# Mamba mixer and mixture of experts on one core: the recurrence's products, the squares and two weight copies moved to GpSimd, the first tap and the output projection moved ahead

## What is computed

```python
def _rmsnorm(x, w, eps=1e-05):
    return x * jax.lax.rsqrt(jnp.mean(x * x, axis=-1, keepdims=True) + eps) * w

def _mamba2_layer(h, Wi, cw, cb, dtb, Alog, Dh, gw, Wo):
    zxbcdt = h @ Wi
    z, xBC, dt = jnp.split(zxbcdt, [D_INNER, D_INNER + CONV_DIM], axis=-1)
    xp = jnp.pad(xBC, ((0, 0), (D_CONV - 1, 0), (0, 0)))
    conv = cb + sum((xp[:, k:k + L, :] * cw[:, k] for k in range(D_CONV)))
    xBC = jax.nn.silu(conv)
    ...
    def step(hs, inp):
        dA_t, dtx_t, B_t, C_t = inp
        hs = hs * dA_t[:, :, None, None] + dtx_t[..., None] * B_t[:, None, None, :]
        y = jnp.einsum('bhpn,bn->bhp', hs, C_t)
        return (hs, y)
    ...
    y = ys.swapaxes(0, 1) + Dh[None, None, :, None] * xs
    y = _rmsnorm(y * jax.nn.silu(z), gw)
    return y @ Wo

for l in range(N_LAYER):
    h = h + _mamba2_layer(_rmsnorm(h, block_norm_w[l]), W_in[l], conv_w[l], conv_b[l], ...)
```

## Time and profile before

| what | value |
|---|---|
| median of 3 runs | 1160.88 us (1157.63 to 1161.12) |
| profiled execution | 1162.99 us, span 1161.0 us |
| mean granted clock of TensorE | 0.952 |
| PE busy | 993.7 us (86%) |
| DVE busy | 977.1 us (84%) |
| ACT busy | 884.2 us (76%) |
| POOL busy | 676.3 us (58%) |

### The profile page before, as it was taken

How to read it: one execution, slowest core, us unless ns; L and a number is a source line. 1 busy time by engine, 2 the same in 40 slices (tenths; PEclk the granted TensorE clock), 3 DMA queues, 4 the chain that set the end, 5 groups by cost and what they waited for, 6 DMA issues and landing times.

```text
span 1161.0 us, 25184 instructions
## 1 busy us (share of the span) xinstructions
PE 993.7 (86%) x6136; PEld 559.7 (48%) x6136; DVE 977.1 (84%) x1801; ACT 884.2 (76%) x1724; POOL 676.3 (58%) x853
## 2 busy tenths in 40 slices
PE   5799999999899999999999999985788767999980
PEld 4244544445444444454445444542444445777760
DVE  6779999999999999999999998974778775888865
ACT  5688999999899999999999999984556534655640
POOL 0267577766776677656655765672244551666661
PEclk9789999999999999999999999998888888999995
DMA  5111242224222432210001000100000115676638
GB/s 141 34 34 33 89 156 86 88 87 153 91 86 87 142 102 86 78 32 22 22 23 31 22 22 23 27 7 1 19 28 28 37 33 180 223 232 226 223 116 217
DMA packets 85584, 97.84 MB, mean 84 GB/s; under 512 B 20698, under 2 KB 65888, under 8 KB 85536
## 3 DMA queue, kind: packets, MB, share of 16 engines
q1 hardware_dynamic: 80544, 88.83, 24.2%
q0 software_dynamic: 4992, 8.48, 2.2%
HBM read 59.67 MB, written 37.83 MB: 84 GB/s over the span
## 4 chain that ended last, share of the span: by engine, by line
PE 35%; DVE 26%; issue 18%; ACT 6%; POOL 3%; DVEq 2%; DMA 1%; ACTq 0%; SPq 0%; POOLq 0%
DVE cv L1354 9%; PE bank L494 4%; PE bank L562 4%; PE bank L681 2%; PE bank L667 2%; DVE M L1370 2%; PE bank L683 2%; PE bank L682 2%; DVE cv L1350 2%; PE bank L619 2%; PE bank L693 2%; PE bank L695 2%; PE bank L692 2%; PE bank L658 2%; PE bank L640 2%
## 5 line engine op out<-in xcount | busy, mean ns | idle before, releaser
L1354 DVE SCALAR_TENSOR_TENSOR cv<-bank,PAR,cv 128x511 f32<-128x511 f32 (+2 forms) x384 | 274.1, 742 | 15.7 <-ACT cv L963 2.8
L1370 DVE SCALAR_TENSOR_TENSOR M<-E,bank 128x512 f32<-128x512 f32 x256 | 168.3, 678 | 20.7 <-ACT E L951 11.4
L1679 POOL TENSOR_TENSOR yt<-yt,ti 128x384 f32<-128x384 f32 x64 | 64.0, 1000 | 203.6 <-DVE ti L1470 203.6
L494 PE MATMUL bank<-hn,WA 128*128 128x512 f32 x256 | 144.9, 649 | 41.0 <-DVE cv L1354 40.6
L951 ACT ACTIVATE E<-bank 128x512 f32<-128x512 f32 x256 | 149.0, 595 | 31.9 <-DVE M L1370 30.1
L1710 POOL DMA_INDIRECT RS<-y,XR x92 | 98.8, 1074 | 78.7 <-DVE y L1567 55.4
L1703 POOL DMA_INDIRECT XS<-stage,IDX x64 | 65.9, 1029 | 79.2 <-DVE run L1329 62.1
L1101 ACT ACTIVATE hr<-bank,W1B 128x512 f32<-128x512 f32 x92 | 63.4, 689 | 56.7 <-PE bank L683 49.8
L562 PE MATMUL bank<-M,dtx 128*32 128x128 f32 x2048 | 82.9, 279 | 15.6 <-DVE o_sb L1389 15.1
L494 PEld LDWEIGHTS bank<-hn,WA 128*128 128x128 f32 x256 | 40.6, 194 | 111.9 <-issue 74.0
L1497 DVE TENSOR_TENSOR hL<-hr,hH 128x512 fp32r<-128x512 f32 x124 | 87.1, 702 | 4.3
(11 more groups left out here) (245 smaller groups left out, 2633.8 us busy)
## 6 DMA issues: line engine op xcount, KB each, us to landing
XS<-PADT SPq DMA_DIRECT2D x32, 520.0 KB, 4.3
WA<-w_in SPq DMA_DIRECT2D x192, 64.0 KB, 1.8
W1B<-WD SPq DMA_DIRECT2D x23, 514.0 KB
W2B<-WD SPq DMA_DIRECT2D x23, 512.5 KB
WD<-WS SPq DMA_DIRECT2D x16, 512.0 KB, 2.7
XR<-XS SPq DMA_DIRECT2D x23, 260.0 KB
RW<-w_in SPq DMA_DIRECT2D x18, 256.0 KB, 4.4
WO_raw<-w_out SPq DMA_DIRECT2D x32, 128.0 KB, 3.6
```

The source lines that it names most:

```text
L494: mm(bank[t % 2][:, :], WA[t][:, :], hn[:, :], start=True, stop=True).then_inc(pj_mm, 1)
L1354: stt(out=cv[t][:, s:L], in0=src[:, 0:L - s], scalar=PAR[:, bass.ds(cw + 3 - s, 1)], in1=cv[t][:, s:L], op0=ALU.mult, op1=ALU.add).then_in ...
L1370: stt(out=M[i % 4][:, :].rearrange("p (n t) -> p n t", n=4), in0=E[i % 2][:, :].rearrange("p (n t) -> p n t", n=4), scalar=1.0, in1=bank[5 ...
```

## The change

- GpSimd makes the two decay products `stmp`, and VectorE the sums. Between the sums VectorE makes the two skip sums: S1, skip sum 0, S2, skip sum 1, S3.
- The first tap on tile 0 of the next unit stands in VectorE's list ahead of the two `ti`, no longer at the head of the next step. In the head, tap 3 on tile 0 is moved ahead of tap 1 on tile 1, and tap 2 on tile 1 behind the causal products.
- GpSimd makes `sqh` (a step earlier than it is needed), `WDT` and `WO`, between `own` and the decay products.
- TensorE's list has the output projection ahead of `project(3)`.
- Semaphores are renamed and counted anew: `s_v` counts 3 to a unit (it was 5), `decay_p` counts the decay products.

```diff
@@ TensorE, body
                 if C and not B:
                     square_mean_of_h(1)
-                if A:
-                    project(3)
                 if C:
                     project_out()
+                if A:
+                    project(3)
@@ ScalarE
-            def norm_square(n):
-                wait(act, dt_mm, n)
-                f(WDT[:, :], PAR[:, bass.ds(n // NB * NPAR + C_WDT, 32)], ACT.Copy).then_inc(wdt_a, 1)
-                wait(act, hup, n + 1)
-                wait(act, ms_mm, n)
-                f(sqh[:, :], h[:, bass.ds(n % NB * L, L)], ACT.Square).then_inc(sqh_a, 1)
...
-                if N:
-                    norm_square(k + 1)
-                elif A:
+                if A and not N:
                     square_h(0)
...
-                    wait(act, s_wo, 16 * (j + 1))
-                    wait(act, out_mm, j)
-                    gw = act.snap(j // NB * NPAR + C_GW)
-                    for t in range(2):
-                        f(WO[:, t * DM:(t + 1) * DM], WO_raw[:, t * DM:(t + 1) * DM], ACT.Copy,
-                          scale=PAR[:, bass.ds(gw + t, 1)]).then_inc(wos_a, 1)
@@ VectorE, body
                 if A:
-                    tap(0, 0)
-                    tap(0, 1)
-                    tap(0, 2)
-                    tap(1, 1)
-                    tap(0, 3)
-                    tap(1, 2)
+                    tap(k, pk, 0, 1)
+                    tap(k, pk, 0, 2)
+                    tap(k, pk, 0, 3)
+                    tap(k, pk, 1, 1)
                 if B:
                     causal_products()
+                if A:
+                    tap(k, pk, 1, 2)
...
                 if B:
+
+                    def with_skip(t):
+                        wait(dve, y_mm, 4 * j + 4)
+                        wait(dve, fin_p, 4 * j - 2 + 2 * t)
+                        stt(out=yt[t][:, :], in0=conv_rows(t, odd + 1), scalar=PAR[:, bass.ds(pj + C_D + t, 1)],
+                            in1=bank[6 + t][:, :], op0=ALU.mult, op1=ALU.add).then_inc(fin_v, 1)
 
                     wait(dve, st_mm, 2 * j + 1)
                     wait(dve, yi_mm, 2 * j)
                     cp(S[1][:, :], bank[4][:, 0:DI]).then_inc(s_v, 1)
-                    wait(dve, dec_a, j + 1)
                     for c in range(2, NC):
-                        wait(dve, s_v, 5 * j + 2 * c - 3)
-                        tt(stmp[:, :].rearrange("p (h d) -> p h d", h=NH), S[c - 1][:, :].rearrange("p (h d) -> p h d", h=NH),
-                           dec[:, (c - 1) * NH:c * NH].unsqueeze(2).to_broadcast([P, NH, HD]), ALU.mult).then_inc(s_v, 1)
-                        wait(dve, s_v, 5 * j + 2 * c - 2)
+                        with_skip(c - 2)
+                        wait(dve, decay_p, 2 * j + c - 1)
...
+                    if N:
+                        tap(k + 1, dve.snap((k + 1) // NB * NPAR), 0, 0)
@@ GpSimd
+            def square_h(n):
+
+                hb = h[:, bass.ds(n % NB * L, L)]
+                wait(pool, hup, n + 1)
+                wait(pool, ms_mm, n)
+                tt(sqh[:, :], hb, hb, ALU.mult).then_inc(sqh_done, 1)
+
+            def step_weights(n):
+
+                wait(pool, dt_mm, n)
+                tt(WDT[:, :], PAR[:, bass.ds(pool.snap(n // NB * NPAR + C_WDT), 32)], ones_row[:, 0:32], ALU.mult).then_inc(wdt_done, 1)
+
+            def output_weights(n):
...
+                    tt(WO[:, t * DM:(t + 1) * DM], WO_raw[:, t * DM:(t + 1) * DM], PAR[:, bass.ds(gw + t, 1)].to_broadcast([P, DM]),
+                       ALU.mult).then_inc(wos_p, 1)
@@ GpSimd, body
                 if A:
                     own_rows(0)
                     own_rows(1)
+                if N:
+                    step_weights(k + 1)
                 if B:
+                    output_weights(j)
+                if N:
+                    square_h(k + 2)
+                if B:
 
+                    wait(pool, dec_a, j + 1)
+                    for c in range(2, NC):
+                        wait(pool, s_v, 3 * j + c - 1)
+                        tt(stmp[:, :].rearrange("p (h d) -> p h d", h=NH), S[c - 1][:, :].rearrange("p (h d) -> p h d", h=NH),
+                           dec[:, (c - 1) * NH:c * NH].unsqueeze(2).to_broadcast([P, NH, HD]), ALU.mult).then_inc(decay_p, 1)
                     for t in range(2):
                         wait(pool, fin_v, 4 * j + 3 + t)
                         tt(yt[t][:, 128:512], yt[t][:, 128:512], ti[t][:, :], ALU.add).then_inc(fin_p, 1)
```

More of the change, by code:

```diff
@@ L446, in square_mean_of_h @@
                 if n == 1:
-                    wait(pe, s_v, 5 * STEPS)
+                    wait(pe, s_v, 3 * STEPS)
                 else:
@@ L616, in body @@
                 if N:
-                    wait(pe, sqh_a, k + 2)
+                    wait(pe, sqh_done, k + 2)
                     wait(pe, zc_a, k + 1)
@@ L652, in body @@
                 if B:
-                    wait(pe, s_v, 5 * j + 5)
+                    wait(pe, s_v, 3 * j + 3)
                     for t in range(2):
@@ L1335, in gate, with tap @@
                 dve.wait_ge(setup_v, 1)
+            def tap(k, first, t, s):
+                cw = first + C_CW + 4 * t
+                src = bank[t % 2]
+                if s == 0:
+                    wait(dve, pj_mm, 6 * k + t + 1)
+                    wait(dve, silu_a, 6 * (k - 1) + SILU_TURN[t] + 1)
+                    ts(cv[t][:, :], src[:, :], PAR[:, bass.ds(cw + 3, 1)], PAR[:, bass.ds(first + C_CB + t, 1)],
+                       ALU.mult, ALU.add).then_inc(tap_v[t], 1)
+                else:
+                    wait(dve, tap_v[t], 4 * k + s)
+                    stt(out=cv[t][:, s:L], in0=src[:, 0:L - s], scalar=PAR[:, bass.ds(cw + 3 - s, 1)],
+                        in1=cv[t][:, s:L], op0=ALU.mult, op1=ALU.add).then_inc(tap_v[t], 1)
             def body(k, odd, A, B, C, N):
@@ L1340, in body @@
                     pk = dve.snap(k // NB * NPAR)
[L1342 to L1355, removed]
                 def causal_products():
@@ L1408, in body @@
                 if A:
-                    tap(1, 3)
+                    tap(k, pk, 1, 3)
                     running_sum()
@@ L1413, in body @@
                 if A:
-                    tap(2, 1)
+                    tap(k, pk, 2, 1)
                 if B:
@@ L1417, in body @@
                 if A:
-                    tap(2, 2)
+                    tap(k, pk, 2, 2)
                 if C:
@@ L1433, in body @@
                 if A:
-                    tap(3, 3)
+                    tap(k, pk, 3, 3)
                 if B:
@@ L1460, in body @@
                         halve(0)
-                    for t in range(2):
-                        if t == 0:
-                            wait(dve, y_mm, 4 * j + 4)
-                        wait(dve, fin_p, 4 * j - 2 + 2 * t)
-                        stt(out=yt[t][:, :], in0=conv_rows(t, odd + 1), scalar=PAR[:, bass.ds(pj + C_D + t, 1)],
-                            in1=bank[6 + t][:, :], op0=ALU.mult, op1=ALU.add).then_inc(fin_v, 1)
+                    if N:
+                        tap(k + 1, dve.snap((k + 1) // NB * NPAR), 0, 0)
                     for t in range(2):
@@ L1579, in expert @@
                         low_slots(i + 1)
+            tap(0, 0, 0, 0)
             steps(dve, body)
@@ L1615, in _ @@
                            channel_multiplier=0).then_inc(padt_p, 1)
+            def square_h(n):
[7 more added lines that the diff above has]
+            def output_weights(n):
+                gw = pool.snap(n // NB * NPAR + C_GW)
+                wait(pool, s_wo, 16 * (n + 1))
+                wait(pool, out_mm, n)
+                for t in range(2):
+                    tt(WO[:, t * DM:(t + 1) * DM], WO_raw[:, t * DM:(t + 1) * DM], PAR[:, bass.ds(gw + t, 1)].to_broadcast([P, DM]),
+                       ALU.mult).then_inc(wos_p, 1)
             def body(k, odd, A, B, C, N, W=None):
```

40 lines of the change are left out of this document (23 added, 17 removed).

## The result

The changed kernel takes 1166.59 us in the median of 5 runs (1165.33 to 1170.67) against 1160.88 (5 runs by now, 1157.63 to 1161.73). The medians lie 5.7 us apart; the ratio over the runs is 1.0056, with a 95% interval of 1.0038 to 1.0075, so the change makes the kernel slower by about half a per cent. The prediction had 1182 us, +21. The profiled execution has a span of 1168.8 us, 7.8 more than before.

A forecast was written before the change was run, and what follows sets the result against it. No engine alone bounded the kernel before; GpSimd's round would bound split steps after. 17 split steps at +0.96 us (16) and 14 others at +0.35 (5) gave +21, 1182 us against 1160.88; range 1158 to 1197.

The forecast's parts named there:

- GpSimd becomes the bound in the split steps: Steps splitting expert weights: GpSimd's round grows to 24.36 us against 23.4, its idle time shrinking to the handoffs.
- part (a) of the prediction: One square, the `WDT` copy and two `WO` scalings move from ScalarE to GpSimd, ahead of the decay products: 2.29 us.
- 0.38 us a split step instead of 0.96: Predicted lengthening of each of 17 steps that split weights: 0.96 us, 16 us in all.
- GpSimd to another engine ... floor 0.05, I take 0.2.: Handoff of each decay product from GpSimd to VectorE's state sum, priced at 0.2 us.
- 0.37 to the first inter-chunk product.: Wait from S3's end to TensorE's first inter-chunk product, 0.37 us of the round's last 1.95 us.
- The upper bound of the round, 24.9: GpSimd's split-step round with 0.23 us for every handoff, 0.73 for a product and 0.40 for `WDT`.
- the steps without a split, -0.04 instead of +0.35: 14 steps without weight splitting: longer tail and TensorE slip, +0.35 us each, 5 us in all.
- I had 6.05 and 6.4: Steps without a split: next tap starts 6.05 us after S1's start, 6.4 behind the branch, against 5.67 and 6.19.
- The Trainium skill's factor of two: GpSimd about twice as slow on two-input elementwise work: a decay product an estimated 0.85 us, 0.44 us a step more.
- That VectorE wins everywhere: Rival: GpSimd's idle time swallows the added work, 31 steps shorten by 0.96 us, -30, 1131 us; chance 0.12.
- That gain and loss cancel: Rival: GpSimd bounds only split steps (+16), the others win 0.96 us each (-13), 1164 us; chance 0.12.
- That it is slower still: Rival: decay product 0.76 us on GpSimd, round 24.6, tail elsewhere +0.55, top 1194 to 1198 us; chance 0.13.

The follow-up runs named there:

- e6: Changed kernel plus one more 128x256 GpSimd product between `own` and the copy of `WDT`, in split steps alone: ratio 1.0151 to the kernel before, split steps 24.32 us.
- e14: Changed kernel with `spend` on GpSimd and nothing else: ratio 1.0100 to the kernel before, split steps 23.97 us, the others 23.10.
- e5: Changed kernel with the first tap back at the head of the step, behind `ti`: ratio 1.0245 to the kernel before, split steps 24.37 us, the others 23.93.
- e4: Changed kernel with both decay products back on VectorE and the skip sums behind S3: ratio 1.0118 to the kernel before, split steps 24.22 us.
- e10: e1 with `spend` written as a two-tensor product with a broadcast operand: ratio 1.0046 to the kernel before, most split steps 23.7 us.
- e2: Changed kernel with the square of the next input back on ScalarE, `WDT` and `WO` still on GpSimd: ratio 1.0033 to the kernel before.
- e7: Changed kernel plus one more 128x256 GpSimd product between `own` and the copy of `WDT`, in steps without a split alone: ratio 1.0064 to the kernel before.
- e12: e1 with `spend` made on GpSimd, behind `wdec`, and off VectorE: 1153.61 us, ratio 0.9941 to the kernel before, all steps 23.10 us.
- e1: Changed kernel with GpSimd's scalings of `WO` and its square moved behind the two decay products: ratio 1.0047 to the kernel before, split steps 23.69 us.

## Why the prediction was right or wrong

**Right: GpSimd becomes the bound in the split steps.** The four instructions of part (a) of the prediction took 402.42 to 404.79, 2.37 us against 2.29 predicted, and they keep the first product waiting behind S1. e6 and e14 show the bound. GpSimd bounds these steps while it is busy for 67% of the span: room in the busy share was no room in the order of time.

**Wrong: the size, 0.38 us a split step instead of 0.96.** Two terms of the sum were mis-sized.
- *"GpSimd to another engine ... floor 0.05, I take 0.2."* It took 0.03 (406.56 to 406.59), and ahead of S2 at most 0.04 (405.40 to 405.44), where VectorE was also just ending the skip sum. The row that I took it from was GpSimd's wait for its own result. Product, sum, product, sum took 404.79 to 407.01, 2.22 us instead of 2.60.
- *"0.37 to the first inter-chunk product."* I read it from S3's end at 402.34 and TensorE's start at 402.71, but there TensorE was still at its early projections (1.98 us from 400.89). Where TensorE waits for S3 it starts 0.06 later. From S3's end to GpSimd's sum with `ti` took 407.01 to 408.67, 1.66 instead of 1.95.

With these the round is 17.56 + 2.33 + 2.22 + 1.66 = 23.77, which is the step of 23.78. (2.33 is from the next step, 426.23 to 428.56.)

The upper bound of the round, 24.9, has a slip besides: its own terms add up to 25.0.

**Wrong: the steps without a split, -0.04 instead of +0.35.** S3 ended 3.25 and 3.18 us after S1 began, in turn, not 3.55, by the same handoffs and because the last within-chunk product ended earlier against S1:

```profile
636.96 0.41 DVE L1442 COPY S<-bank 128x256 f32<-128x256 f32 x1
...
642.38 3.18 DVE L1335 SCALAR_TENSOR_TENSOR cv<-bank,PAR,cv 128x511 f32<-128x511 f32 x4
...
660.05 0.41 DVE L1442 COPY S<-bank 128x256 f32<-128x256 f32 x1
661.00 0.75 DVE L1437 SCALAR_TENSOR_TENSOR yt<-xbc,PAR,bank 128x512 f32<-128x512 f32 x1 [0.54 <-PE bank L562]
...
662.81 0.42 DVE L1449 TENSOR_TENSOR S<-stmp,bank 128x256 f32<-128x256 f32 x1
...
665.68 0.75 DVE L1335 SCALAR_TENSOR_TENSOR cv<-bank,PAR,cv 128x511 f32<-128x511 f32 x1 [0.19 <-issue]
```

From S3's end to the end of the second `ti` it was 2.26 us, not 2.47: the mis-sized 0.37 again. So the tail from S1 to the second tap took 5.42 us (636.96 to 642.38) and, in the step with the loop's branch, 5.63 (660.05 to 665.68), against 5.68 and 6.18 before; I had 6.05 and 6.4. The branch now leaves VectorE idle for 0.19 us, where it was 0.40 ahead of the first tap; in e5, with the tap behind `ti` again, the steps without a split differ in turn by half a microsecond once more (24.17 and 23.68). What the tail gives, the rest of the step takes back, as I had it in kind but not in size: from the second tap to S1 17.67 us (642.38 to 660.05) and 17.48, where the kernel before has 17.22 (637.60 to 654.82) and 17.24:

```profile
631.92 0.43 DVE L1447 COPY S<-bank 128x256 f32<-128x256 f32 x1
...
637.60 3.62 DVE L1354 SCALAR_TENSOR_TENSOR cv<-bank,PAR,cv 128x511 f32<-128x511 f32 x5
...
654.82 0.42 DVE L1447 COPY S<-bank 128x256 f32<-128x256 f32 x1
```

The chain now runs through GpSimd's `y2` (the chain in order of time: start, length, what):

```profile
645.43 1.29 POOL y L1704
646.74 0.64 ACT sqy L995
647.38 0.12 issue
647.50 1.12 PE bank L503 x2
648.62 0.86 PE bank L504 x2
649.48 0.86 PE bank L510 x2
```

TensorE waits 0.39 us for that square. The tail, 0.4 us shorter in the mean, and the rest of the step, 0.35 longer, add up to almost no change; e4, with the products on VectorE, comes to 23.15.

**Missed: contention.** I had looked for stretched rows on GpSimd and found 0.10 us. The stretched rows were on VectorE, in the trace of before: `spend` (the 128x32 scaling of e10's edit) 743 ns in the mean of the split steps and 233 without (groups by line, the window 100 to 440 us, then 610 to 730 us; behind the bar the busy time and the mean ns of one):

```profile
L1383 DVE TENSOR_SCALAR spend<-CST,p 128x32 bf16<-128x32 f32 x14 | 10.4, 743 | 0.0
...
L1383 DVE TENSOR_SCALAR spend<-CST,p 128x32 bf16<-128x32 f32 x5 | 1.2, 233 | 0.0
```

After, the group of 100 to 440 us is this:

```profile
L1369 DVE TENSOR_SCALAR spend<-CST,p 128x32 bf16<-128x32 f32 x14 | 16.8, 1198 | 0.0
```

because the two lists stand differently to each other: `spend` now starts with the second split product. Busy time counts such a hold as work. The Trainium skill ("GPSIMD Engine Reference", Key points) names contention with VectorE instructions in a two-port mode or with two inputs in SBUF. The trace agrees for instructions with two tensor inputs in SBUF: `spend` in its two-tensor form (1.29 us for 0.18, e10), the decay product (816 ns for 425, e4) and `hn` (1.09 us for 0.75). `spend` as a scaling has one such tensor and is held too (1.26 us for 0.23); in which mode it ran no run shows.

**The Trainium skill's factor of two** for elementwise work on GpSimd ("GPSIMD Engine Reference", Engine selection) was set against a row of 630 ns; the moved product took 616 on GpSimd against 425 on VectorE. The row was the better price.

**The rivals.** That VectorE wins everywhere fell with the wait for the within-chunk product (0.54 to 0.85 us in the rows above). That gain and loss cancel came nearest in time and is half right: no loss outside the split, but next to no gain either. That it is slower still fell with the price of the product, 0.62 us instead of its 0.76, and with the handoffs.

## What to carry to other kernels

Before a wait is priced from the gap between a producer and its consumer, look at what the consumer did in that gap: here it was still working, and the wait proper was 0.06 us. Work moved to an engine with idle time belongs behind the instructions that others wait for, and that alone was worth only 0.1 us because a second bound lay that close; compare both kinds of steps before and after. Group an instruction's durations by stretch: one whose length changes while its shape does not is being held. Whether the hold costs anything only an experiment tells: on `hn` it cost nothing, since VectorE waited behind it anyway (e2, e7), and on `spend` 0.6 us a step (e12 against e1), more than the change at hand.

## What the runs showed of the hardware

- A VectorE instruction of 32 columns with its operands in SBUF lasted until the end of the GpSimd instruction beside it in nearly every split step: 1.26 us for 0.23, ending within 0.05 us of it (418.00 and 417.98; 415.71 and 415.66), as a scaling and as a two-tensor product alike. In two steps of e10 it was not held (0.18 us), and GpSimd's instruction took 1.34 us instead of 1.27.
- Both sides can be stretched: GpSimd's two scalings of `WO` take 1.20 us beside `hn`, and `hn` 1.03, where alone they take 0.76 and 0.75. With one more product ahead of them `hn` took 1.66 (e7).
- From GpSimd to VectorE a handoff took 0.03 us, from VectorE to TensorE 0.06. GpSimd's spans in a profile are rough, and the first of these is a difference of such spans.
